# Order of group 0's norm, group 1's sum and two gate weights in the prologue of a two-layer graph network kernel

## What is computed

```python
y = adj @ x[b]                                  # per batch
h = h0 = layernorm(x + (y @ W0 + b0))
for _ in range(3):
    a = adj @ h                                  # in_mat and out_mat are both adj
    z = sigmoid([a, a] @ w3.T + b3 + h @ u3.T + bu3)
    r = sigmoid([a, a] @ w4.T + b4 + h @ u3.T + bu3)
    v = tanh([a, a] @ w5.T + b5 + (r * h) @ u5.T + bu5)
    h = (1 - z) * h + z * v
out = layernorm(h0 + h)
```

## Time and profile before

| | us |
|---|---|
| median of 3 runs | 1592.21 (1592.07 to 1592.35) |
| time of the profiled execution | 1592.15 |
| its span, first to last instruction | 1590.4 |
| TensorE busy | 1578.3 (99%) |
| VectorE busy | 1404.9 (88%) |
| ScalarE busy | 1184.2 (74%) |
| GpSimd busy | 264.6 (17%) |

### The profile page before, as it was taken

One profiled execution on the slowest core, in us unless ns is written; L12 is line 12 of the kernel. 1 busy time (PEld: TensorE's weight loads), 2 busy tenths in 40 slices (PEclk: granted clock), 3 DMA queues, 4 the chain that ended last, 5 costly groups with the idle time before them and its releaser, 6 DMA issues.

```text
span 1590.4 us, 21729 instructions
## 1 busy us (share of the span) xinstructions
PE 1578.3 (99%) x7114; PEld 1312.7 (83%) x7114; DVE 1404.9 (88%) x1523; ACT 1184.2 (74%) x2474; POOL 264.6 (17%) x307
## 2 busy tenths in 40 slices
PE   9999999999999999999999999999999999999997
PEld 9888888888888888888888888888888888888885
DVE  7988888998889888899888998889998899878888
ACT  5677767787777877777786777777787777876666
POOL 5100101121111221112111111101112021110023
PEclk9999999999999999999999999999999999999999
DMA  5555546776567675687656776566765677555444
GB/s 194 174 177 182 190 154 210 240 238 215 180 202 244 224 234 157 220 244 235 215 163 217 235 246 199 181 213 226 251 190 194 215 230 232 174 157 189 169 159 159
DMA packets 233491, 323.20 MB, mean 203 GB/s; under 512 B 23201, under 2 KB 198690, under 8 KB 233378
## 3 DMA queue, kind: packets, MB, share of 16 engines
q1 hardware_dynamic: 232960, 321.49, 63.1%
q10 hardware_dynamic: 418, 0.33, 0.1%
HBM read 162.86 MB, written 158.86 MB: 202 GB/s over the span
## 4 chain that ended last, share of the span: by engine, by line
PE 97%; ACT 1%; DVE 1%; DMA 1%; SPq 0%; issue 0%; POOL 0%; ACTq 0%; DVEq 0%; POOLq 0%
PE ps_r L523 48%; PE ps_h L523 32%; PE ps_al L632 8%; PE ps_al L580 4%; PE ps_al L599 2%; PE ps_al L589 1%; SPq L352 0%; PE ps_al L613 0%; PE ps_al L567 0%; DMA h_scratch_a<-h_blocks_a 0%; PE ps_al L705 0%; PE ps_al L547 0%; DMA h_landed_a<-h_scratch_a 0%; PE ps_h L547 0%; PE ps_h L567 0%
## 5 line engine op out<-in xcount | busy, mean ns | idle before, releaser
L754 ACT ACTIVATE rh_hi<-rh 128x512 fp32r<-128x512 f32 x192 | 118.8, 633 | 146.7 <-DVE rh L1250 146.7
L1222 DVE STREAM_TRANSPOSE a_blocks<-ps_al 128x1024 f32<-128x1024 f32 x92 | 114.1, 1240 | 120.7 <-PE ps_al L632 120.4
L966 ACT ACTIVATE z_sb<-ps_r,bias_z 128x512 f32<-128x512 f32 x192 | 127.6, 682 | 68.1 <-PE ps_r L523 67.8
L954 ACT ACTIVATE rh<-ps_r,bias_r 128x512 f32<-128x512 f32 x192 | 128.9, 683 | 59.6 <-PE ps_r L523 54.6
L1068 DVE TENSOR_TENSOR rh_lo<-rh,rh_hi 128x512 fp32r<-128x512 f32 x192 | 125.0, 689 | 9.3
L970 ACT ACTIVATE hv<-ps_h,bias_h 128x512 f32<-128x512 f32 x192 | 121.2, 677 | 10.9 <-PE ps_h L523 10.9
L1262 DVE TENSOR_TENSOR hv<-hv,z_sb 128x1024 f32<-128x1024 f32 x95 | 116.4, 1225 | 9.9
L1502 POOL TENSOR_TENSOR h_var_eps_sb<-x_spread,eps 128x4 f32<-128x4 f32 x28 | 6.4, 230 | 702.5 <-ACT h_nat_h L797 119.5
L523 PE MATMUL ps_r<-a_hi_a,w_hi 128*128 128x512 f32 x384 | 118.5, 390 | 0.1
L523 PE MATMUL ps_r<-h_hi,u_hi 128*128 128x512 f32 x384 | 118.4, 390 | 0.0
L523 PE MATMUL ps_r<-a_hi_a,w_lo 128*128 128x512 f32 x384 | 118.3, 389 | 0.0
(11 more groups left out here) (414 smaller groups left out, 4179.1 us busy)
## 6 DMA issues: line engine op xcount, KB each, us to landing
h_scratch_a<-h_blocks_a SPq DMA_DIRECT2D x48, 512.0 KB, 4.3
h_landed_a<-h_scratch_a SPq DMA_DIRECT2D x192, 128.0 KB, 2.9
h_scratch_b<-h_blocks_b SPq DMA_DIRECT2D x47, 512.0 KB, 4.3
h_landed_b<-h_scratch_b SPq DMA_DIRECT2D x188, 128.0 KB, 2.9
a_scratch_a<-a_blocks SPq DMA_DIRECT2D x46, 512.0 KB, 2.7
a_landed<-a_scratch_a SPq DMA_DIRECT2D x184, 128.0 KB, 2.9
a_scratch_b<-a_blocks SPq DMA_DIRECT2D x46, 512.0 KB, 2.7
a_landed<-a_scratch_b SPq DMA_DIRECT2D x184, 128.0 KB, 2.8
```

What stands on the lines that cost most here:

```text
L754: return act.activation(dst, src, ACT.Copy)
L954: act.activation(rh[:, c, :], ps_r[:, c, :], ACT.Sigmoid, bias=bias_r[:, c:c + 1]).then_inc(r_ready, 1)
L966: act.activation(z_sb[:, c, :], ps_r[:, c, :], ACT.Sigmoid, bias=bias_z[:, c:c + 1]).then_inc(z_ready, 1)
L1222: tr = dve.transpose(flat_blocks(a_blocks).rearrange("p (x e) -> p x e", e=Q), flat(ps_a).rearrange("p (x f) -> p x f", f=Q))
```

## The change

It moves instructions and alters none. On ScalarE, `first_norm(0)` stands ahead of `first_graph_high(2)`, and `first_norm(1)` behind `gate_high("w5")`. On VectorE, `graph_low(0)`, the low parts of w4 and u3 and the three sums of the gates' biases stand ahead of `first_sum(1)`. On GpSimd, the sum of w3's halves and the subtraction stand ahead of `first_scale(1)` and `add_bias(3)`.

```diff
@@ ScalarE
             first_graph_high(1)
+            first_norm(0)
             first_graph_high(2)
-            first_norm(0)
...
             state_high(0)
-            first_norm(1)
             act.wait_ge(gate_sum["w5"], 1)
             gate_high("w5")
+            first_norm(1)
@@ VectorE
             first_graph_low(2)
             first_blocks(0)
-            first_sum(1)
             graph_low(0)
             gate_low("w4")
             gate_low("u3")
+            dve.wait_ge(gate_bias_in, 16)
+            dve.tensor_tensor(bias_z[:, :], bias_in[:, 0, :], bias_in[:, 3, :], ALU.add)
+            dve.tensor_tensor(bias_r[:, :], bias_in[:, 1, :], bias_in[:, 3, :], ALU.add)
+            dve.tensor_tensor(bias_h[:, :], bias_in[:, 2, :], bias_in[:, 4, :], ALU.add).then_inc(biases_ready, 1)
+            first_sum(1)
             first_graph_low(3)
             state_low(0)
             first_sum(2)
...
             gate_low("w3")
             gate_low("u5")
-            dve.wait_ge(gate_bias_in, 16)
-            dve.tensor_tensor(bias_z[:, :], bias_in[:, 0, :], bias_in[:, 3, :], ALU.add)
-            dve.tensor_tensor(bias_r[:, :], bias_in[:, 1, :], bias_in[:, 3, :], ALU.add)
-            dve.tensor_tensor(bias_h[:, :], bias_in[:, 2, :], bias_in[:, 4, :], ALU.add).then_inc(biases_ready, 1)
@@ GpSimd
             add_halves("w5")
-            first_scale(1)
-            add_bias(3)
             add_halves("w3")
             pool.wait_ge(gate_sum["w4"], 1)
             pool.wait_ge(gate_sum["w3"], 1)
             pool.tensor_tensor(gate_raw["w3"], gate_raw["w3"], gate_raw["w4"], ALU.subtract).then_inc(gate_sum["w3"], 1)
+            first_scale(1)
+            add_bias(3)
             first_scale(2)
```

## The result

| | before | after |
|---|---|---|
| median (5 runs each) | 1592.35 (1592.07 to 1592.76) | 1598.50 (1598.06 to 1600.66) |
| profiled execution | 1592.15 | 1598.06 |
| its span | 1590.4 | 1596.3 |
| TensorE busy | 1578.3 | 1579.9 |

The change makes the kernel slower: the ratio of after to before is 1.0042, with a 95% interval of 1.0031 to 1.0052 (a ratio is taken over the single executions and differs a little from that of the two medians). 1598.4 was predicted.

The account below looks back on a forecast made before the run. TensorE, 99% busy and almost never waiting, was taken as the bound. The profiled 1592.15 + 4.45 (late first_graph(3) under full queueing) + 1.8 (clock fall) gave 1598.4 us, range 1593.8 to 1600.6.

Parts of the forecast that it names:

- Place and releaser: TensorE idle 4.7 us ahead of line 547's matmuls (first_graph(3)), released by VectorE's line 1167, group 1's addition.
- The bare order: VectorE's new order without queueing behind GpSimd: first_sum(1) at 22.38 us, first_graph(3) at 23.62, 1.88 us late.
- ScalarE's part: Norm 0 ahead of group 2's copy: graph(0) at 16.53 us, 0.44 gained, 0.16 lost again at first_weights(2).
- GpSimd beside it: GpSimd's w5 and w3 sums and subtraction delay VectorE's SBUF instructions; first_graph(3) shift grows from 1.88 to 4.45 us.
- The full queue: Upper bound, every SBUF instruction queues: first_graph(3) 4.45 us late; chance 0.46 with clock fall, 0.24 without.
- Taking turns: VectorE and GpSimd alternate whole instructions when both wait, from w5's sum ending at 21.33 us to the bias sums.
- the two bounds: Shift of first_graph(3): +1.88 us with no queueing, +4.45 us with the full queue.
- The clock: TensorE's clock falls about when it resumes at first_graph(3); costs 0 to 1.84 us, 1.8 taken.
- my doubled price: Clock cost behind the pause up to twice as large if the low stretch lasts twice as long.
- the likelier of two cases: With the full queue, TensorE's clock falls (1598.4 us, chance 0.46) or stays (1596.6 us, chance 0.24).
- What is late next: Behind first_graph(3) no further stall; h_lo may end at 33.6 us for 34.54, reserve 0.9; further-stall rival 0.07.

Follow-up runs that it names:

- GpSimd held back: Changed kernel with GpSimd made to wait for group 1's addition before the sum of w3's halves: 1594.68 us, ratio 1.0014.
- the run with the bias sums back: Changed kernel with the three bias sums at their old place on VectorE: 1596.56 us, ratio 1.0027; run once more for its trace, 1596.19 us.
- the run with a busy pause: Changed kernel with 20 unused adjacency matmuls on TensorE between first_weights(2) and the wait of first_graph(3): 1596.24 us, ratio 1.0024.
- the two that were written to have none: ScalarE's new order kept, VectorE reordered with group 1's statistics later: 1593.35 us; the same with the bias sums early too: 1592.65 us.

## Why the prediction was right

**Place and releaser.** Confirmed: a single pause in the prologue, ahead of line 547 on group 3's rows, released by line 1167.

**The bare order.** +1.88 us was the sum. VectorE's order alone gave 1594.55 - 1592.45 = 2.1, since without ScalarE's part `graph_low(0)` starts some 0.3 us later. With GpSimd held back it was 2.2, of which some 0.4 is the stretch of w4's part; without that, 1.8.

**GpSimd beside it.** The full queue gave 24.95 us for `first_sum(1)` and 26.19 for `first_graph(3)`; measured 24.92 and 26.28, and this trace runs 0.18 us behind the one of before from the load of x on (w5's sum 20.20 against 20.02). Taking turns was inferred from one short instruction of before; the ends above alternate just so, and holding GpSimd back takes 2.25 us off (2.13 with both traces counted from w5's sum); with the 0.4 by which w5's sum still stretches w4's part that is the 2.57 between the two bounds. I had w4's part at 0.9 and u3's at 1.7 us; they are 1.09 and 1.74. The Trainium skill (SBUF — State Buffer, "Who interferes with whom") says that a VectorE instruction with at most one SBUF input, outside the 2-port modes, does not contend with GpSimd; the run with the bias sums back agrees, with 1.21 us for the addition beside a working GpSimd.

**The clock.** 1.8 us was taken, between 0 and 1.84. The profiled execution shows 1.5 us, so this term was some 0.3 too large there. Its price came from the first matmuls, which were read as running at the low level by their double duration alone: the granted clock reads 1.00 over the first matmuls in every trace here, so no row shows the level there. In the changed kernel clock and duration stand side by side, 0.50 and 3.46 us for 16 passes. The medians give more than 1.5: 2.3 us against the run with a busy pause. Two of the five executions, 1599.66 and 1600.66 us, have a mean granted clock of 0.995 instead of 0.997; my doubled price (up to 3.7) could describe these, though no trace of them was taken, so the longer low stretch in them is argued from the mean alone. That the clock would fall at all was called the likelier of two cases, from 4.5 us at the tail. By time and mean clock (1597.94 us, 0.996) it may have fallen once behind a pause of 2.1 us, which the prediction had called well short of that; no trace shows it, and it made no difference to the sum.

**ScalarE's part.** The step was right (no idle time ahead of `graph(0)`, `first_weights(2)` held by group 2's low part), but I charged it with a gain of 0.28 us. In the changed kernel that is so. It starts `graph(0)` at 16.54 us (16.72 less the 0.18 from the start), where 16.53 was forecast. Alone it comes to a loss of 1.2 us between medians, because of w4's low part, which the prediction never looked at, since in the new order it comes early.

**What is late next.** No second pause appeared in the prologue; the 0.2 us at 1445 us were not foreseen. `h_lo` took 1.38 us and ended at 33.4, for a product at 36.14; I had feared 33.6 for 34.54, and the low clock gave it more time.

**How much of the agreement is luck.** The mechanism is right, but the 0.1 us between 1598.4 and the median is not to be read as its precision. Between the two profiled executions the difference is 1598.06 - 1592.15 = 5.9 us, where 4.45 + 1.8 = 6.25 was forecast: the shift was 4.36 (4.54 less the 0.18 from the start) and the clock took 1.5. The five executions then spread over 2.6 us, and their median happens to lie 0.44 us above the profiled one.

## What to carry to other kernels

Where one engine never waits, look for waits that are met with time to spare before you move anything: the reuse of a PSUM bank was 2.2 us from being a stall and showed in no list of waits. Check each moved instruction also against what GpSimd does at that moment: two subtractions and three tiny sums with both operands in SBUF held VectorE for 4.0 us (20.95 to 24.92) in place of 1.4, because GpSimd had large sums ready. And price a stall of TensorE above its length, since the clock may fall in it; here 4.5 us of waiting became 6. A list of instructions without that pause is not yet a better one: the two that were written to have none came out no faster than the kernel before.

## What the hardware showed that was not expected

- A sum over 128x2 elements took 1.21 us instead of 0.15 behind a GpSimd instruction and ended 0.01 us after it: what it waited for was the end of the other's instruction, whatever its own size.
- A part of the differences between executions comes from the start. The first eight matmul passes of line 547 took 1.07 us in one trace (the busy pause), 1.92 in another (the single run with the bias sums back) and 1.49 in the kernel before, and what follows shifts with them (w5's sum on GpSimd: 19.61, 20.78 and 20.02 us). That the clock rises earlier or later beneath them would explain it, but the granted clock reads 1.00 there in all three.
- With pauses of 2.1 and 3.2 us the clock stayed up in the profiled executions. Some of the timed ones, up to 3.4 us longer and with mean clocks of 0.995 or 0.996 in place of 0.998, look as if it fell in them; no trace of one was taken.
- Two of 13 executions of one kernel took 2682 and 3256 us. The first had a granted clock of 0.556 from the first 4 us on. The second, 2.04 times the normal time, is recorded with 1.0 and has no trace. What set them off is open.
